# Score products in 32x32 tiles in token order, exponential after the transpose, value products split by output partitions, output by token, edge labels on GpSimd, the two halves of the batch interleaved

## The reference, cut to what matters

```python
# block 0: transformer block with conditioning, 16 heads of 8 features
shift_msa, scale_msa, gate_msa, shift_mlp, scale_mlp, gate_mlp = split(silu(c) @ w_ada + b_ada, 6)
k, q, v = split(modulate(ln(x), shift_msa, scale_msa) @ w_qkv, 3)
y = softmax(q @ k.T / 8) @ v                    # per sample and head, 32 x 32 scores
x = x + gate_msa * (y @ w_proj + b_proj)
h = gelu(modulate(ln(x), shift_mlp, scale_mlp) @ w_mlp1 + b_mlp1)   # 512 wide
x = x + gate_mlp * (h @ w_mlp2 + b_mlp2)
# block 1: graph attention, 16 heads, two directions, keys are the first 20 tokens
self_feat = concat(x, cond, or 0 where the sum of a row of x is 0) @ W_self.T + b_self
output = self_feat
for d in range(2):
    A = adj if d == 0 else adj with its two token axes swapped      # int32, 11 labels
    A = A[:, :, :20]
    s = (q_d @ k_d.T) / sqrt(8), or -9e15 where A.sum(-1) == 0
    s = s + (A @ w_bias + b_bias)
    output = output + (softmax(s) @ kv) @ Wout_d.T + bout_d         # kv: first 20 tokens
return x + relu(output)
```

## Time and profile before

| | value |
|---|---|
| device time, median of 3 runs | 135.92 us |
| the three runs | 135.62, 135.92, 139.38 us |
| span of the profiled execution, first to last instruction | 137.4 us |
| mean granted TensorE clock of it | 0.898 of full speed |
| PE busy / weight loads busy | 102.6 us (75%) / 76.3 us (56%) |
| DVE busy | 92.2 us (67%) |
| ACT busy | 80.1 us (58%) |
| POOL busy | 56.6 us (41%) |
| DMA | 5.78 MB, mean 42 GB/s |
| the chain that ended last, by engine | PE 37%, ACT 23%, DVE 22%, issue 11%, DMA 2%, POOL 2% |

### The profile page before, as it was taken

How to read it: one execution, slowest core, us unless ns; L and a number is a source line. 1 busy time by engine, 2 the same in 40 slices (tenths; PEclk the granted TensorE clock), 3 DMA queues, 4 the chain that set the end, 5 groups by cost and what they waited for, 6 DMA issues and landing times.

```text
span 137.4 us, 3252 instructions
## 1 busy us (share of the span) xinstructions
PE 102.6 (75%) x1238; PEld 76.3 (56%) x1238; DVE 92.2 (67%) x224; ACT 80.1 (58%) x196; POOL 56.6 (41%) x70
## 2 busy tenths in 40 slices
PE   0396899269968580485899989799699697699651
PEld 0383778169946430231444456678498596598540
DVE  5797995941986899816444088789875748426880
ACT  3009679966595150033032889969959969837511
POOL 7269999999991699102000001222422322402000
PEclk9999999955999959559999999999999999856985
DMA  4996000000000000334000000000000000000004
GB/s 133 423 417 258 0 2 0 0 7 0 5 0 5 0 0 0 34 97 110 0 0 5 0 0 0 0 0 5 2 5 2 5 0 5 0 0 5 5 4 148
DMA packets 4543, 5.78 MB, mean 42 GB/s; under 512 B 2480, under 2 KB 3632, under 8 KB 4272
## 3 DMA queue, kind: packets, MB, share of 16 engines
q1 hardware_dynamic: 4096, 4.52, 9.8%
q10 hardware_dynamic: 432, 1.05, 2.0%
HBM read 4.88 MB, written 0.69 MB: 41 GB/s over the span
## 4 chain that ended last, share of the span: by engine, by line
PE 37%; ACT 23%; DVE 22%; issue 11%; DMA 2%; POOL 2%; ACTq 0%; DVEq 0%; POOLq 0%
ACT Vz L635 11%; PE ps_t L578 7%; PE ps_s L568 6%; PE ps_d L520 5%; PE ps_d L524 5%; DVE masked L766 4%; PE ps_d L459 4%; DVE xn_tok L709 4%; PE ps_y L589 4%; ACT PT L681 3%; ACT E L676 3%; ACT Kz L624 3%; DVE stats L698 3%; DMA x_tok<-in_x_tok 2%; PE ps_d L536 1%
## 5 line engine op out<-in xcount | busy, mean ns | idle before, releaser
L450 POOL TENSOR_TENSOR E<-E,neg_max 128x320 f32<-128x320 f32 x15 | 10.9, 726 | 49.9 <-DVE neg_max L884 49.9
L568 PEld LDWEIGHTS ps_s<-Kz,Qm 128*128 128x128 f32 x192 | 26.6, 213 | 2.2 <-issue 1.4
L568 PE MATMUL ps_s<-Kz,Qm 128*128 128x80 f32 (+1 forms) x192 | 27.7, 294 | 0.1
L635 ACT ACTIVATE Vz<-ps_d 20x128 f32<-20x128 f32 (+1 forms) x96 | 25.7, 267 | 2.3 <-PE ps_d L497 1.1
L578 PE MATMUL ps_t<-ident,E 128*128 128x128 f32 x96 | 16.8, 303 | 6.7 <-ACT PT L681 5.1
L681 ACT ACTIVATE PT<-ps_t 128x512 f32<-128x512 f32 x24 | 14.3, 596 | 12.8 <-PE ps_t L578 12.6
L645 ACT ACTIVATE hidden<-ps_d,cols 128x512 f32<-128x512 f32 x8 | 5.4, 686 | 19.8 <-PE ps_d L520 19.8
L578 PEld LDWEIGHTS ps_t<-ident,E 128*128 128x128 f32 x96 | 11.5, 154 | 9.0 <-ACT E L676 5.7
L589 PE MATMUL ps_y<-Vz,PT 128*32 128x36 f32 x768 | 12.0, 210 | 4.4 <-ACT Vz L635 1.8
L589 PEld LDWEIGHTS ps_y<-Vz,PT 128*32 128x32 f32 x768 | 9.3, 120 | 8.3 <-ACT PT L681 3.8
L520 PE MATMUL ps_d<-xm,w_rest_sb 128*128 128x512 f32 x16 | 9.5, 724 | 5.7 <-DVE xm L718 5.2
(11 more groups left out here) (96 smaller groups left out, 188.8 us busy)
## 6 DMA issues: line engine op xcount, KB each, us to landing
Qm<-in_adj SPq DMA_DIRECT2D x1, 1408.0 KB, 8.4
w_rest_sb<-in_w_rest SPq DMA_DIRECT2D x1, 1088.0 KB, 10.6
bias_rep<-bias_dram SPq DMA_DIRECT2D x4, 160.0 KB, 3.0
x_tok<-in_x_tok ACTq DMA_DIRECT2D x2, 256.0 KB, 3.6
xT<-in_xT ACTq DMA_DIRECT2D x1, 512.0 KB, 5.4
w_ada_sb<-in_w_ada SPq DMA_DIRECT2D x1, 384.0 KB, 4.3
out<-x_tok SPq DMA_DIRECT2D x1, 256.0 KB, 2.3
w_qkv_sb<-in_w_qkv SPq DMA_DIRECT2D x1, 192.0 KB, 5.6
```

The source lines that it names most:

```text
L450: pool.tensor_tensor(e, e, nm.unsqueeze(2).broadcast_to([P, UB * HQ, M]), ALU.add)\
L568: ins = pe.matmul(ps_s[i % 2][:, b * P:b * P + HQ * nk], Qm[d][:, g * UB + b, :, :], Kz[d][:, g * UB + b, :, 0:nk], start=True, stop=True)
L635: ins = act.activation(Vz[d][QUAD * hq:QUAD * hq + nk, h * BH + b:(h + 1) * BH:UB, :, hq * C:(hq + 1) * C], src[:, :, hq, :, :], ACT.Copy)
```

## The change

- Scores: query and key layouts swap roles. Queries are plain (`q0T`, `q1T`, one copy per dense product); keys are masked four ways (`Kb0`, `Kb1`, all 128 partitions). A unit has 16 products of 32 rows by 32 columns of weights, one for each sample b and each feature quarter j. Row quarter j of the array writes bank j of the new four-bank `ps_s`; a partition of the result is (sample, query). There is one such `ps_s` instead of two banks in turn.
- The transpose comes before the exponential. ACT's exponential reads `ps_t` and writes `PT`; exp (L676) is gone and copy (L681) becomes it. The unused columns of `E1` hold -30000 instead of 0.
- Values: `ps_y` is one bank instead of two. The v products are split into 32 output partitions each (`HI` column tiles), so that ACT needs 4 pieces per product instead of 16. Both directions of block 1 share one product of 64 columns per sample.
- The bias now has the layout of the scores: no transfer through DRAM. POOL does the labels on int32 in 12 steps of `ORDER`, its mask too; DVE only makes the other direction (`edges`).
- Output by token: POOL adds the output bias to selfT (`selfb`) and y0 to it (`ya`); ACT takes two transposes per half (`sbtok`, `x2tok`); DVE does `ysum` and `relu` per group, and SP stores from that.
- POOL subtracts the maximum in all 16 units of block 1.
- `ps_d` has two banks, assigned by the table `BANKS`, instead of three.
- `ORDER` is new and finer (recip, mult, badd, max, sub, stats, rstd, apply, shift, label, zero are steps of their own). It interleaves the second half's block 0 with the first half's mlp, and the second half's mlp with units 8 to 11.

```diff
+    ("take", (("x1tok", 0), 0)), ("label", 8), ("scores", 7), ("values", 5), ("max", 7), ("label", 9),
+    ("dense", ("xn2T", 0)), ("label", 10), ("turn", 6), ("exp", 6), ("take", (("xn2T", 0), 0)), ("label", 11),
+    ("sub", 7), ("turn", 7), ("exp", 7), ("shift2", 0), ("dense", ("mlp1", 0, 2)), ("take", (("mlp1", 0, 2), 0)),
...
+    ("take", (("k1", 0, 0), 3)), ("scores", 8), ("take", (("mlp1", 1, 2), 0)), ("badd", 8), ("dense", ("sbtok", 0)),
+    ("take", (("sbtok", 0), 0)), ("dense", ("mlp1", 1, 1)), ("take", (("mlp1", 1, 1), 0)), ("dense", ("mlp1", 1, 0)),
...
+ACT_PARTS = {
+    "k": (0, 1, 2, 3), "v": (0, 1, 2, 3), "v1": (0, 1, 2, 3), "qz": (0,), "yT": (0,), "mlp1": (0,), "x2tok": (0,),
+    "sbtok": (0,), "q1": (0,), "k1": (0, 1, 2, 3),
+}
...
+        ps_s = ctx.enter_context(nc.psum_tensor("ps_s", [P, HJ, 512], F32))
...
                     for b in range(UB):
-                        ins = pe.matmul(ps_s[i % 2][:, b * P:b * P + HQ * nk], Qm[d][:, g * UB + b, :, :],
-                                        Kz[d][:, g * UB + b, :, 0:nk], start=True, stop=True)
+                        for j in range(HJ):
+                            q = slice(QUAD * j, QUAD * j + QUAD)
+                            ins = pe.matmul(ps_s[QUAD * b:QUAD * b + QUAD, j, 0:HI * nk], qT[q, g * UB + b, :],
+                                            Kb[q, g * UB + b, :, :], start=True, stop=True)
...
+                    if i >= 1:
+                        pe.wait_ge(scores_read, i)
...
+                assert kind == "v1"
+                b0, w = h * BH + name[2] * BH // 2, DIRS * HJ * C
+                for b in range(BH // 2):
+                    for i in range(HI):
+                        ins = pe.matmul(ps[QUAD * i:QUAD * i + M, b * w:(b + 1) * w], selfT[:, b0 + b, 0:M],
+                                        w_v1[:, i, :], start=True, stop=True)
...
-                    act.activation(E[:, i % 3, :, 0:nk], E[:, i % 3, :, 0:nk], ACT.Exp).then_inc(exp_ready, 1)
-                elif stage == "copy":
                     act.wait_ge(turned, i + 1)
...
-                    act.activation(PT[:, i % 2, :, :], ps_t[:, :].rearrange("p (b t) -> p b t", t=P), ACT.Copy)\
+                    act.activation(PT[:, i % 2, :, :], ps_t[:, :].rearrange("p (j t) -> p j t", t=P), ACT.Exp)\
                        .then_inc(pt_ready, 1)
...
+                    elif i < L:
+                        pool.tensor_scalar(label_tmp[:, i % 2, :], a, wb[:, i:i + 1], 0.0, ALU.mult, ALU.add)\
+                            .then_inc(pool_own, 1)
...
+                        pool.tensor_tensor(label_sum[:, i % 2, :], before, a, ALU.add).then_inc(pool_own, 1)
...
+                        pool.tensor_tensor(label_bias[:, i % 2, :], label_bias[:, (i - 1) % 2, :],
+                                           label_tmp[:, i % 2, :], ALU.add).then_inc(pool_own, 1)
...
+                elif stage == "ya":
...
+                    pool.tensor_tensor(ya[:, i, :], y0[:, i, :], sb_tok[:, i, :], ALU.add).then_inc(ya_ready, 1)
...
+                elif stage == "ysum":
...
+                    dve.tensor_tensor(y0[:, i, :], y1[:, i, :], ya[:, i, :], ALU.add).then_inc(ysum_ready, 1)
+                elif stage == "relu":
...
+                    dve.scalar_tensor_tensor(out=out_tok[:, i, :], in0=y0[:, i, :], scalar=0.0, in1=x2_tok[:, i, :],
+                                             op0=ALU.max, op1=ALU.add).then_inc(out_ready, 1)
```

More of the change, by code:

```diff
@@ L36 @@
 QUAD = 32
-HQ = 4
-H4 = 4
+HI = 4
+HJ = 4
+H = HI * HJ
 C = 8
@@ L504, in dense_product @@
                 if kind == "yT":
-                    pe.wait_ge(y_ready, (h + 1) * UH)
+                    pe.wait_ge(y_ready, max(UNITS.index((0, 0, h * UH + u)) for u in range(UH)) + 1)
                     return turn4(ps, lambda i: y_tok[:, h * UH + i, :])
@@ L580, in _ @@
+                    for j in range(HJ):
+                        ins = pe.transpose(ps_t[:, j * P:(j + 1) * P], E[:, i % 3, j * HI:(j + 1) * HI, :], ident[:, :])
                     ins.then_inc(turned, 1)
@@ new lines, in take_part @@
+                if kind == "v1":
+                    act.wait_ge(vz_ready[1], 1)
+                    q = slice(QUAD * part, QUAD * part + M)
+                    b0 = h * BH + name[2] * BH // 2
+                    return act.activation(
+                        Vz[q, b0:b0 + BH // 2, :, :, part * C:(part + 1) * C].rearrange("p b d j c -> p (b d j) c"),
+                        ps[q, :].rearrange("p (n c) -> p n c", c=C), ACT.Copy)
+                assert kind in ("x2tok", "sbtok")
+                act.wait_ge(bias_ready, 1)
@@ new lines, in take_part @@
+                if kind == "k":
+                    return dve.tensor_scalar(Kb0[:, bs, part, :], ps_bs, head_mask[:, 0, part:part + 1], None, ALU.mult)
+                if kind == "v":
+                    dve.wait_ge(vz_ready[0], 1)
+                    q = slice(QUAD * part, QUAD * part + QUAD)
+                    return dve.tensor_copy(Vz[q, bs, 0, :, part * C:(part + 1) * C],
+                                           ps[q, :].rearrange("p (b j c) -> p b j c", j=HJ, c=C))
+                if kind in ("proj", "mlp2"):
+                    dve.wait_ge(taken_dve, DVE_TAKES.index((("cmod", 1), 0)) + 1)
+                    bias, gate = (R_PROJ, 2) if kind == "proj" else (R_MLP2, 5)
+                    return dve.scalar_tensor_tensor(out=gated[:, bs, :], in0=ps_bs, scalar=cols[:, bias:bias + 1],
+                                                    in1=over_s(cmod, gate, bs), op0=ALU.add, op1=ALU.mult)
@@ new lines, in take_part @@
+                if kind == "self":
+                    dve.wait_ge(taken_dve, DVE_TAKES.index((("rowsum", h), 0)) + 1)
+                    return dve.scalar_tensor_tensor(out=selfT[:, bs, :], in0=ps_bs, scalar=cols[:, R_SELF:R_SELF + 1],
+                                                    in1=zeroed_q[:, :, :], op0=ALU.add, op1=ALU.add)
+                if kind == "q1":
+                    d = name[2]
+                    return dve.tensor_scalar(q1T[d][:, bs, :], ps_bs, cols[:, R_Q + d:R_Q + d + 1], None, ALU.add)
```

922 lines of the change are left out of this document (440 added, 482 removed), and 21 rows, old and new, of tables (BANKS, ORDER, UNITS).

## The result

The changed kernel takes 125.12 us (median of 4 runs, 122.78 to 126.73) beside 137.45 of the kernel before on the same chip (4 runs, 135.62 to 139.38). The ratio is 0.909, with an interval of 0.897 to 0.921. A later set of four on another chip had 124.12 and 0.904. The change makes the kernel about 9% faster; the forecast was 109.5, its range ended at 121, and so the gain is less than half of the 26 us foretold. The profiled execution took 124.52 us with a span of 122.6. Most kernels here have some executions that are 2 to 3% longer at a lower granted clock; the ratios and their intervals leave these out, the medians don't, and where too few others were left a median stands without a ratio.

The account below looks back on a forecast made before the run. Bound by the order in which four engines hand work over, PE nearest its limit. First scores 14, block 1's first scores 57, last stage 49.8 to 107, end 3.5: span 110.5, scaled and rounded to 109.5 us; range 102 to 121.

Parts of the forecast that it names:

- The conversion: Whole kernel: span of 110.5 us times 135.92/137.4 gives a median time of 109.3, rounded to 109.5.
- The start: Before first scores: POOL's added zero-filling puts first rstd at 7.1 us and first scores at 14, up from 12.5.
- Block 0's attention, and the way to block 1's first scores: Stages after first scores: block 0's attention ends at 42 us, block 1's first scores come at 57, bounds 52 and 62.
- DVE leads: Block 0's attention: DVE is the busiest engine with 23.8 us, ahead of ACT's near 15.
- At 85% of busy time the stage takes 28 us: Block 0's attention: DVE's 23.8 us at 85% busy make 28 us, where 36.5 were before.
- The last stage: Block 1's 16 units with half 1's mlp: PE's 44.8 us at 90% busy take 49.8 us, to 107.
- PE loses score time: Attention scores: a unit's 32 small records cost PE 0.50 us, bounds 0.40 and 1.11, instead of 1.06 in block 1.
- the rival of row tiles that don't overlap: Scores: row tiles don't run side by side, a unit costs PE 1.11 or 1.78 us; time near 128; chance 0.12.
- The labels: POOL's label steps: 23 to 30 us, ending at 40 to 48, before `edges` near 45; otherwise a stall up to 3.
- No DVE instruction near 5 us: Sign of being right: the 5.65 us DVE stall behind POOL's zero-filling, ahead of mlp1, goes whole.
- I cost both at nothing: Block 1's units: scores waiting for badd's read of `ps_s`, and the like cycle of values, reciprocal and multiplication, cost nothing.
- The other rivals: ACT and two `ps_d` banks block PE, 8 us, 117.5, chance 0.15; low clock after PE idles, near 142, chance 0.04.

Follow-up runs that it names:

- merged: Changed kernel with one value product per sample instead of four, 1152 fewer PE instructions, three quarters of attention outputs from wrong scores; 115.85 us, ratio 0.853.
- start: Changed kernel with half 1's zero-filling moved from POOL's first steps to the middle of block 0's attention; 123.31 us, ratio 0.905.
- start_fill: Changed kernel with start's moved zero-filling and 32 tiny idle products at the head of PE's program; 120.22 us, ratio 0.884.
- seq: Changed kernel with half 1's mlp, row sum and self products all before block 1's first step; 136.08 us, ratio 0.989.
- exp_back: Changed kernel with the exponential again an ACT step of its own on E, directly before the transpose; 139.27 us, ratio 1.024.
- exp_back2: Changed kernel with the exponential again an ACT step of its own, directly behind the subtraction; 132.41 us, ratio 0.965.
- v_old: Changed kernel with v's dense products at 128 output columns again, 16 ACT pieces instead of 4; 125.41 us, ratio 0.914.

## Why the prediction was wrong in size

**The conversion.** I scaled a span of 110.5 by 135.92/137.4 to 109.3. The profiled execution of before was the one of 139.38 us, not the median; time is span plus 1.9 to 2.0 in both kernels (139.38 with 137.4, 124.52 with 122.6). The same span would have been 112.4 as the time of one execution: 3.1 us of the 15.2 that the profiled execution lies over the sum. The other 12.1 are span. For the median the conversion did little harm, by luck: 112.4 x 135.92/139.38 is 109.6. But all my rows come from an execution at a mean clock of 0.898, where those of the same kernel up to 136.2 us had 0.949 to 0.962.

**The start** gave 15.2 instead of 14, with the first rstd at 8.16 instead of 7.1. I had read in the earlier trace rows that a DVE instruction of a few hundred elements waits out POOL's zero-filling, priced the memsets moved to the start at POOL's own time alone, and did not look at which DVE steps would run beside them.

**Block 0's attention, and the way to block 1's first scores**, 56.2 us for 43, is the larger part, and only about half of it is found. `merged` reaches those scores 2.6 us earlier and `start` 3.3; `start_fill`, with the start mended and 1.9 us less of the waits near 30, still reaches them at 66.3 and not at 57. That stretch takes 52.7 us in it, against 43 forecast, with PE busy 41.3 and DVE 33.8. The two waits of the supply near 30 us are 3.5 of the 13.2 too much. One error of placing is visible in the trace: six mlp1 products run before 71.4, and I had put all four of half 1 behind. The two are 2.1 us, with half 1's transposes around them. The clock is a third part. I took four mlp1 products at the full clock; the first two ran at the lower of its levels:

```profile
42.00:44.00 2.00, 0.53 (x40) 0.34 (x42) 1.62 (x10) 0.20 (x1) 1.28 (x2) 1.00 0.00 0
...
48.00:50.00 2.00, 2.00 (x6) 0.83 (x4) 0.42 (x2) 1.25 (x2) 1.91 (x4) 0.50 0.00 0
...
48.49 1.92 PE L515 MATMUL ps_d<-xm,w_rest_sb 128*128 128x512 f32 x2
...
50.97 1.96 PE L515 MATMUL ps_d<-xm,w_rest_sb 128*128 128x512 f32 x2
...
56.48 1.05 PE L515 MATMUL ps_d<-xm,w_rest_sb 128*128 128x512 f32 x2
```

That is 1.8 us. The step "DVE leads" and "At 85% of busy time the stage takes 28 us" failed: DVE was busy 24.3 us, about the 23.8 that I had summed, in 33.3 (73%). The stage is led by no engine, and dividing the busiest one by a share that fits a saturated stage made it too short. What fills the remaining 5 to 6 us, hand-overs among four engines by the look of it, stays open.

**The last stage** came out at 48.0 for 50, by luck, and for a reason I did not give. PE's work was 41.0 for 44.8, half of the difference being the two products just named and the other half the full clock and cheaper scores. But PE at "90%" needed a cause for the other 10%, and I took hand-overs. What stood in its place was a count: 2777 matmul and weight-load records with PE's semaphore instructions, at about 15 ns each, are 43 us, more than PE's busy time. The step that failed is "PE loses score time", which counts a unit's 32 records at 0.50 us and nothing for issuing four times as many as before. By `merged`, the count costs 6.5 us here and 7 to 9 of the whole, and with it gone the time (115.85) is inside the range.

**Right:** scores of 0.42 to 0.53 us a unit (0.61 and 0.62 in two units of block 0 at a lowered clock, one in block 1 cut by a wait); the rival of row tiles that don't overlap is refuted. The labels, complete at 51.6 us, are 6.5 us ahead of `edges` at 58.1, and POOL's scalar label steps took 0.54 us on average, within the bounds (the last one took 1.08). No DVE instruction near 5 us, two of 2.5. Interleaving half 1's mlp works, and by `seq` is worth 11 us, nearly the whole net gain.

**"I cost both at nothing"** was right for the extra wait on `ps_s`, of which no trace shows a stop of its own. The transposed exponential I credited with the last unit's latency alone; `exp_back` and `exp_back2` give it 8 to 15 us in this order. They measure it in an order that was written for the short path; what it was worth against the order of before, no run shows, so it can't be set against the sum.

**The other rivals.** ACT's key and value pieces hardly stopped PE: the longest waits of the last stage fall on block boundaries. With 13.6 us more on ACT (`v_old`) they begin to count. The clock did not decide: its mean is 0.951 and 0.964 in two executions of the changed kernel, and 0.949 to 0.962 in those of the one before up to 136.2 us. It fell to 0.50 twice: from 36 to 38 us, after the waits of the supply (PE busy 0.65 and 1.05 of 2 us in the windows from 32 to 36), and from 46 to 52, after PE had been busy 0.53 and 1.04 of 2 us in the windows from 42 to 46. It stood at 1.00 in the last stage, where the waits are 0.4 to 1.2.

## What to carry to other kernels

Count instructions as well as busy time when a product is split into small tiles: 16 tiles in place of 4 products may cost the array half the time and still lose to the supply of instructions; compare the instructions of a stage, weight loads and semaphores included, times what a block costs (here 15 ns for each) with the stage's length, and look at the packets of the instruction queue. An idle time with no releaser that recurs every 256 instructions is the sign of it, and a few idle products at the start are a cheap test. Keep a short ACT step off the path between two PE steps when ACT's queue holds pieces of 0.6 us, and keep POOL's large memsets away from small TENSOR_SCALAR steps of DVE. A stage that no engine leads is not its busiest engine divided by 0.85.

## What the runs showed of the hardware that was not expected

PE waits of 0.4 to 2.3 us at fixed positions 256 instructions apart, with a pace of 3.7 to 4.0 us per 256 where work is dense, whatever the instructions are: scores, values, transposes. Between the waits the pace reached 6 ns for each, and the next packet started 1.0 to 1.4 us after PE went on. Sixteen row and column tiles of 32x32 with 80 columns each overlap to 0.45 us a unit (32 records of 240 ns). A TENSOR_SCALAR of 4 elements on DVE took 2.49 us beside two POOL memsets of 3.98 us together, and 0.17 without; a TENSOR_REDUCE beside them took 0.23.
